# A macaron block on one core: new orders of events, and a down projection that reads its weights where they lie

## What is computed

```
x = x + 0.5 * ffn(layernorm(x))
x = x + attn(layernorm(x), keys, values)          # 16 heads of 8, 512 keys, relu projections, plus its own input
x = x + 0.5 * ffn(layernorm(x))

def ffn(x):                                       # 8 experts of 256, the best 2 of each token
    probs = softmax(norm(x) @ gate_w.T)
    w = the two largest of probs, over their sum plus EPS
    out = swiglu(x, sWg, sWu, sWd)                # the shared expert
    for e in range(8):
        out = out + w[:, e:e+1] * swiglu(x, Wg[e], Wu[e], Wd[e])
swiglu(x, g, u, d) = (silu(x @ g) * (x @ u)) @ d
```

## Time and profile before

| | |
|---|---|
| median of 3 runs | 910.74 us (908.45 to 915.92) |
| the profiled execution | 916.63 us |
| its span, first to last instruction | 914.8 us |
| TensorE busy | 751.5 us |
| VectorE busy | 635.6 us |
| ScalarE busy | 530.6 us |
| GpSimd busy | 479.9 us |

### The profile page before, as it was taken

The page is one execution under the profiler, slowest core; times in us unless marked ns, Lnnn a source line. Parts: engine busy times, 40 slices in busy tenths (PEclk is TensorE's granted clock), DMA queues, the critical chain, the costliest instruction groups (busy, mean ns, idle before and its releaser), DMA issues.

```text
span 914.8 us, 17245 instructions
## 1 busy us (share of the span) xinstructions
PE 751.5 (82%) x5089; PEld 471.0 (51%) x5089; DVE 635.6 (69%) x1460; ACT 530.6 (58%) x892; POOL 479.9 (52%) x618
## 2 busy tenths in 40 slices
PE   3589899988969888888888868878897898869881
PEld 2546689888833333333333323323225578759880
DVE  6456656666767898889699957978933555646663
ACT  4552334443436888888878868767884244425440
POOL 8577567767625244334317472274440573746552
PEclk9999999997967999999999989988998998989996
DMA  7322232352130000000001110001110221224434
GB/s 229 124 82 75 76 91 81 85 155 76 45 97 1 8 20 7 20 8 12 16 4 32 33 33 8 8 27 33 54 40 19 63 73 48 80 86 114 135 94 142
DMA packets 71763, 55.57 MB, mean 61 GB/s; under 512 B 14516, under 2 KB 64965, under 8 KB 71670
## 3 DMA queue, kind: packets, MB, share of 16 engines
q1 hardware_dynamic: 62454, 36.61, 14.7%
q0 software_dynamic: 9216, 17.86, 5.8%
HBM read 29.36 MB, written 24.79 MB: 59 GB/s over the span
## 4 chain that ended last, share of the span: by engine, by line
PE 47%; DVE 20%; ACT 12%; issue 8%; DVEq 6%; POOL 3%; SPq 2%; DMA 2%; POOLq 0%; ACTq 0%
PE psum L858 10%; DVE neg_max L1318 9%; PE psum L805 8%; ACT probs L956 7%; DVEq L1275 5%; PE psum L745 4%; PE psum L788 4%; PE psum L755 4%; PE psum L825 3%; PE psum L781 3%; DVE w_gu L1288 3%; PE psum L678 2%; PE psum L741 2%; PE psum L751 2%; DVE w_down L1294 2%
## 5 line engine op out<-in xcount | busy, mean ns | idle before, releaser
L1318 DVE TENSOR_REDUCE neg_max<-psum 128x1 f32<-128x512 f32 x512 | 335.3, 683 | 66.7 <-PE psum L825 59.7
L956 ACT ACTIVATE probs<-psum 128x1024 f32<-128x1024 f32 x256 | 255.7, 1026 | 69.2 <-PE psum L805 65.3
L1412 POOL DMA_INDIRECT slot_rows<-zrow,slot x128 | 130.1, 1016 | 78.9 <-issue 35.2
L825 PE MATMUL psum<-k_stack,q_parts 32*128 32x512 f32 x506 | 132.5, 517 | 32.4 <-DVE neg_max L1318 31.6
L805 PE MATMUL psum<-q_full,k_stack 32*128 32x512 f32 x512 | 126.1, 498 | 28.7 <-ACT probs L956 22.6
L858 PE MATMUL psum<-probs,v_pad 128*32 128x512 f32 x1024 | 142.9, 632 | 0.3
L805 PEld LDWEIGHTS psum<-q_full,k_stack 32*128 32x128 f32 x512 | 49.2, 189 | 167.0 <-ACT probs L956 105.4
L1266 DVE TENSOR_TENSOR work<-work,psum 128x512 f32<-128x512 f32 x112 | 75.6, 679 | 72.0 <-PE psum L781 40.9
L931 ACT ACTIVATE work<-psum 128x512 f32<-128x512 f32 x112 | 66.8, 597 | 91.5 <-PE psum L745 55.4
L1418 POOL DMA_INDIRECT result_rows<-yrow,zslot x80 | 82.2, 1028 | 58.5 <-ACT yrow L939 39.4
L1418 POOL DMA_INDIRECT result_rows<-yrow,probs x80 | 81.6, 1020 | 52.9 <-ACT yrow L939 31.7
(11 more groups left out here) (181 smaller groups left out, 961.2 us busy)
## 6 DMA issues: line engine op xcount, KB each, us to landing
zrow<-result_rows SPq DMA_DIRECT2D x32, 256.0 KB, 4.2
zslot<-slot_rows SPq DMA_DIRECT2D x80, 72.0 KB
probs<-slot_rows SPq DMA_DIRECT2D x80, 72.0 KB
slot_rows<-padrow SPq DMA_DIRECT2D x34, 72.0 KB, 1.7
x<-in_x SPq DMA_DIRECT2D x8, 256.0 KB, 4.0
slot_rows<-zrow,slot POOLq DMA_INDIRECT x128, 2.3
acc<-acc SPq DMA_DIRECT2D x64, 32.0 KB
acc<-recip SPq DMA_DIRECT2D x32, 64.0 KB
```

Of the source, the lines that this page charges most:

```text
L825: mm(bank(M_BANK[m % 3]), q_parts[rows, u % 2, qt * P:(qt + 1) * P], k_stack[rows, u % HI, :], start=True, stop=True).then_inc(m_filled, 1)
L956: nc.scalar.activation(probs[:, k % PRING, 2 * jp:2 * jp + 2, :], psum[:, b:b + 2, :], ACT.Exp, scale=float(DH) ** -0.5).then_inc(s_freed, 1)
L1318: reduce(neg_max[:, u % 2, qt, j:j + 1], bank(b), AX.X, ALU.max, negate=True).then_inc(m_freed, 1)
L1412: nc.gpsimd.indirect_dma_start(d["zd"], bass.IndirectOffsetOnAxis(ap=slot[:, k, tau:tau + 1], axis=0), zrow[:, k, tau, :], None).then_inc( ...
```

## The change

The copies into `w_down`, their buffer and their semaphore are gone. TensorE loads the expert's number from the table into a register itself, and the down projection's moving operand is read from `w` at that address:

```diff
                     G = what[1]
-                    pe.wait_ge(down_copied, (G + 1) * BLK)
+                    q, t = divmod(G, NT)
                     for b in range(BLK):
+                        e = pe.value_load(table[0:1, q % 2, 1, BLK * t + b:BLK * t + b + 1], min_val=1, max_val=NE)
                         for i in range(2):
                             last = mm(psum[:, Y_BANK[n % 2], b * H:(b + 1) * H], h[:, k % 2, (i * BLK + b) * CELL:(i * BLK + b + 1) * CELL],
-                                      w_down[:, G % 2, b, i * H:(i + 1) * H], start=i == 0, stop=i == 1)
+                                      w[:, bass.ds(e, 1), 2 * INTER + i * H:2 * INTER + (i + 1) * H].rearrange("p a c -> p (a c)"), start=i == 0, stop=i == 1)
```

```diff
-        first += [("IDS",)] + turns(0)
+        first += [("IDS",)] + turns(0) + spread_z(1) + sum(turn_of(1, 0), [])
         for n in range(FIRST_BATCHES):
-            z, t = (spread_z(n + 1), turns(n + 1, False)) if n + 1 < FIRST_BATCHES else ([], [])
-            first += route_of(n, R0) + z[:GT] + ([("KEYS",)] if n == 3 else []) + [("EX", n)] + z[GT:] + t[:2] + [("POS", n)] + t[2:]
-            first += ([("BD", 0, g) for g in BATCHES[n + 1][1]] if t else []) + route_of(n, R1)
+            first += route_of(n, R0)
+            if n + 1 < FIRST_BATCHES:
+                z, logit = turn_of(n + 1, 1)
+                first += z + [("EX", n)] + logit + [("POS", n)] + [("BD", 0, g) for g in BATCHES[n + 1][1]]
+            else:
+                first += [("EX", n), ("POS", n), ("KEYS",)]
+            first += spread_z(n + 2) if n + 2 < FIRST_BATCHES else []
+            first += route_of(n, R1)
             first += scatters(0) if n == 0 else [("CNT", 0)] if n == 1 else tabulate_of(0, TB) if n == 2 else [("CNT", 1)]
-        first += [("KV",)] + scatters(1)
-        split = [("KS", 0), ("KS", 1), ("KS", 2), ("KW", 0), ("KW", 1)]
+            first += sum(turn_of(n + 2, 0), []) if n + 2 < FIRST_BATCHES else []
+        first += [("KV",), ("KW", 0), ("KW", 1)] + scatters(1)
+        split = [("KS", 0), ("KS", 1), ("KS", 2)]
```

```diff
-        early_m = maxima(0) + maxima(1)[:2]
+        early_m = maxima(0) + maxima(1)
-        for G, evs in ((NT + 6, [("CB", 0)] + [("MOM", 0, t) for t in range(GT)]), (NT + 7, [("LN", 0)]), (NT + 8, [("CB", 1)]), (NT + 9, [("Z", 0)]),
-                       (NT + 10, [("YT", 0), ("CB", 2)]), (NT + 12, [("PROJ", 0), ("CB", 3)]), (NT + 14, early_m[:1]), (NT + 15, early_m[1:2]),
+        for G, evs in ((NT + 4, [("CB", 0)] + [("MOM", 0, t) for t in range(GT)]), (NT + 5, [("LN", 0)]), (NT + 6, [("CB", 1)]), (NT + 7, [("Z", 0)]),
+                       (NT + 9, [("YT", 0), ("CB", 2)]), (NT + 11, [("PROJ", 0), ("CB", 3)]), (NT + 13, early_m[:1]), (NT + 14, early_m[1:2]),
...
-            m = maxima(k + M_LEAD)
+            m = maxima(2 * k + 4) + maxima(2 * k + 5) if k < 2 else maxima(k + M_LEAD)
...
-        attention += (maxima(0) + maxima(1))[E:] + maxima(2) + maxima(3) + [("MT", 0), ("PROJ", 2)] + maxima(4) + maxima(5)
+        attention += (maxima(0) + maxima(1))[E:] + maxima(2) + maxima(3) + [("MT", 0), ("PROJ", 2)]
```

```diff
-        chain = {("H", 1, 1): turns(m), ("H", 1, 2): [("RECIP", NG - 1)], ("H", 1, 3): route_of(m, 8), ("H", 1, 4): route_of(m, R0 - 8),
-                 ("H", 1, 5): [("EX", m), ("POS", m)], ("H", 1, 6): r_m[:6], ("H", 1, 7): r_m[6:] + sc[0:1], ("H", 1, 8): [("POST", NG - 1)] + sc[1:3],
+        chain = {("H", 1, 1): za, ("H", 1, 2): la + zb, ("H", 1, 3): [("RECIP", NG - 1)] + lb + [("BD", 1, g) for g in BATCHES[m][1]], ("H", 1, 4): route_of(m, 8),
+                 ("H", 1, 5): route_of(m, R0 - 8) + [("EX", m)], ("H", 1, 6): [("POS", m)], ("H", 1, 7): [("POST", NG - 1)] + r_m,
...
-        for at, evs in ((0, z[:2] + sc[6:7]), (1, z[2:] + sc[7:8]), (2, turns(n)), (3, route_of(n, 5)), (4, route_of(n, 5)), (5, route_of(n, 5)),
-                        (6, [("EX", n), ("POS", n)]), (7, r_n[:4]), (8, r_n[4:8]), (9, r_n[8:] + [("CNT", 3)]), (10, sc_n[0:1] + tb[0:3]),
-                        (11, sc_n[1:2] + tb[3:6]), (12, sc_n[2:3] + tb[6:9]), (13, sc_n[3:4] + tb[9:12]), (14, tb[12:])):
+        for at, evs in ((0, [("ZT", 1, NG - 1)] + sc[5:6]), (1, [("LG", n, NG - 1), ("BD", 1, NG - 1)] + sc[6:7]), (2, route_of(n, 8) + sc[7:8]),
+                        (3, route_of(n, R0 - 8) + [("EX", n)]), (4, [("POS", n), ("CNT", 3)]), (5, r_n[:6]), (6, r_n[6:] + tb[:3]), (7, tb[3:7] + sc_n[0:1]),
+                        (8, tb[7:11] + sc_n[1:2]), (9, tb[11:] + sc_n[2:3]), (10, sc_n[3:4])):
```

**SyncE.** The pads of pass 3 come after tile 11's loads, as those of pass 1 did already, and half of the last loads and stores go to ScalarE's queue:

```diff
-                if ph == 0:
-                    load_tiles(0, 0, 12)
-                    pad(1)
-                    load_tiles(0, 12, NT)
-                else:
-                    load_tiles(2, 0, NT)
-                    pad(3)
+                load_tiles(2 * ph, 0, 12)
+                pad(2 * ph + 1)
+                load_tiles(2 * ph, 12, NT)
...
+            for G in range(4 * NT - YRING, 4 * NT):
+                act.wait_ge(slot_out[G % YRING], landed(G))
+            for g in range(PG, NG):
+                load_result(act, g, 1)
+            for g in range(PG, NG):
+                store_half(act, g, 1)
```

47 lines of the change are left out of this document (24 added, 23 removed).

## The result

The changed kernel takes 888.35 us (median of 4 runs, 887.70 to 891.62), the kernel before 913.33 in 4 runs. The ratio is 0.9738, 95% interval 0.9682 to 0.9795: 2.6% faster. The profiled execution took 888.04 us (span 886.2), where 916.63 minus 32 gave 884.6. Of the forecast gain of 32 us, 28.6 came. On the median's footing the forecast was 879, built on the 910.74 of three runs; the median came 9 us above it, inside the likeliest case's range of 866 to 893.

The account below looks back on a forecast made before the run. TensorE was busy 751.5 of 914.8 us, with VectorE's weight copies lengthening most tiles and GpSimd close behind. Terms summed to -32: 884.6 us profiled, 879 on the median's footing; range 863 to 922, likeliest case 866 to 893.

Parts of the forecast that it names:

- rival A: TensorE's register chain in the down projection shows instead of being hidden: 927 us, or 1015 if nothing overlaps; chance 16%.
- B: Relief lost to GpSimd, a longer start, the pads' wait and remaining waits: 21 us less gain, 900 us; chance 18%.
- C: The w_down copies were hidden anyway and the new orders cancel: within 1% of 910.7 us; chance 6%.
- Parts 1 and 8: Dropping w_down copies frees 1.5 us of VectorE per tile; 825 to 896 us nears 2.90 per tile: -9.
- Part 2: Down projection: TensorE's register loads and arithmetic, 1.7 us per tile, hidden by its sequencer's lead; +2, range 0 to 136.
- Part 3: Start, 0 to 90 us: the new order delays the first half and the scatters; net +4, between 0 and +9.
- Part 5: 187 to 252 us: waits for VectorE's product and GpSimd's a_z go, with half-speed tiles; -11, between -6 and -13.
- Parts 4, 6 and the end: 84 to 187 us, GpSimd becomes the bound: -3; 684 to 776, two waits go: -10; last result loads: -1.
- the transition to the attention: After 252 us: loses two maxima, runs eight others beside the first scores, pays part back on VectorE; -2.
- Part 6: 684 to 776 us: TensorE's waits for ScalarE's z copy and VectorE's chosen go; -5 each, together -5 to -12.
- Part 7: 776 to 825 us: pads delay slot loads, a new 13 us wait replaces the old 7.20; 47 instead of 49, -2.

Follow-up runs that it names:

- Experiment 2: The changed kernel with the w_down copies put back (new orders, old down projection): ratio 1.0067 to the kernel before, span 917.7 us.
- Experiment 6: The changed kernel with each of TensorE's register loads done twice: ratio 1.0430 to the kernel before, span 946.4 us.

## Why the prediction was right, and where it was off

The sum, -32, came as -28.6, each part with its sign. Of rival A little was seen, 5.0 us, and no gap of 0.5 us between down matmuls (the longest was 0.35). Of B, the waits on GpSimd and the longer start came, at a part of their price. Of C one half is not excluded: the copies were not hidden, but by the ratios the orders may cancel.

**Parts 1 and 8** (VectorE's copies make the tiles 3.2 to 4.4): shown. In place alone gives 22.0 us and T20' to T39' at 56.4; with orders alone that stretch stays at 67.1. The last 20 tiles are 2.90 each on average, forecast -9, measured -10.1. Experiment 2 shows one thing more: from T3' to T10' the new order makes the copies dearer, 8.9 us where they cost 4.2.

**Part 2** (the chain is hidden, +2, range to 136): the mechanism was right and the margin near (0.6 for 0.5); it showed 5.0 us in 17 gaps, in 11 of the 80 tiles, more than the 2. The prediction had one cause, a late h beside extra work on VectorE. It is there in T25, T3' and T8', and for T0, T2 and T3 h was late beside halves: the load started 0.04 us after h in each. In T15, T16 and T9' it was the transposes ahead of the load that came late, and behind the last tile of each phase there are no matmuls to hide under. Experiment 6 shows that the margin is real and small: rival A was one load per block away. The Trainium skill's floor of some 600 ns for such a load (page "DMA: Bandwidth & Descriptors", section "Latency and other measured facts") is twice what TensorE shows, median 300 ns. By an estimate from the page's figure two loads would lengthen the chain by 0.6 us, the whole margin. Its page "Advanced Engine Details and Errata", section "Sequencer Loop", says that other instructions are read while control instructions execute: the trace agrees up to the lead of this place, some 2 us from the wait ahead of the chain (808.04) to the first down matmul (810.02), and experiment 6 shows where that ends.

**Part 3** (start, +4): +5.3. I had the keys' place as a cost of TensorE alone, a late first half given back in part. The pacing list is a second one: by it GpSimd's scatters wait for the last positions, which the new order puts before the keys. The loads of T0's rows went out at 85.7 in place of 80.0. It was to be read from the lines on pacing.

**Part 5** (T24 to T39, -11, range -6 to -13): -5.9, the term that failed: it is 5 us short, more than the 3.4 by which the sum is off. (Its own sum was off too: 65 less 52.9 is 12.1, not 12.9.) I moved both waits out of the way and kept GpSimd's sum of 63.5 us beside it as a warning. The wait for a_z stayed at 3.62 (3.20 before), with slow matmuls behind it; although its transposes now stand two tiles behind it in place of one, it is late by as much as before, behind GpSimd's moments and copies of results.

**Parts 4, 6 and the end:** -2.0, -10.6 and -1.1 against -3, -10 and -1. For the transition to the attention, -2, the -3.1 measured is within what that stretch varies by. The wait for ScalarE's copy of z is gone, that for chosen of the last batch too. Part 6's waits are where the trace shows a gain of the orders: H to T9' gives 4.8 in place alone, 10.6 with the orders.

**Part 7** (a new wait of 13 us in T10', none at T18): 12.24 and none. Its sum, 47, was 48.5. What the part did not see is that another place on SyncE was better, and none of the three tried is free: over 11 tiles of 2.90 us, T9' to T20' takes 16.6 us more with the pads behind 12 loads, 12.7 behind 17, and 9.6 between the loads.

Of the orders' worth, the timings say less than the traces: 0.9738 for the change and 0.9741 for its in-place half have intervals of 0.6% to either side. That the orders add 6.6 us to it stands in one profiled execution each; by the ratios it is anything from a loss of 8 us to a gain of 8, and stays open. What is shown of the whole is that reading the weights in place gives about 2.6%.

## What to carry to other kernels

A copy that exists only to give another engine a fixed address can go, if that engine's sequencer runs ahead by more than load and arithmetic take. Measure the lead at a wait instruction next to the place, set it against the chain up to the last address, and do not spend it twice; where something ahead of the chain in the queue comes late, the chain shows on top. Work taken off one engine pays at once where it was the bound. Here new orders that put more work of that engine into single tiles were slower before the relief; whether they pay after it is not shown by the totals. Where a queue has fixed work between transfers, such as eight pads, try its place: in a block it held up one tile for 7 to 12 us, and one by one it cost less in sum and spread over six. What paces another engine's queue has to be read again whenever the order of events changes.
